# Order of the two kinds of score products, and of the gating layers, in an attention and routing pipeline

## The reference, cut to what matters

```python
x = x + tanh(g_xattn) * attention(layernorm(x), ctx, ctx)   # 32 query heads, 8 key/value heads, 16 wide
x = x + tanh(g_ffn)   * experts(layernorm(x))               # 8 experts, the best 2 of each token
# attention: softmax(q k^T / 4) v, softmax over the 128 context rows
# experts:   logits = tanh(x Wg1^T) Wg2^T; top 2, softmax of the two; silu(x Wup^T + bup) Wdown^T + bdown
```

## Time and profile before

| | |
|---|---|
| runs | 796.14, 796.16, 802.58 us; median 796.16 |
| profiled execution | 791.42 us, span 789.6 us |
| PE busy | 675.6 us, 86% of the span |
| DVE busy | 551.0 us, 70% |
| ACT busy | 380.1 us, 48% |
| POOL busy | 293.7 us, 37% |
| chain that ended last | PE 69%, DVE 14%, DMA 8%, POOL 3%, issue 3% |
| mean granted clock of PE | 0.946 of full speed |

### The profile page before, as it was taken

How to read it: one execution, slowest core, us unless ns; L and a number is a source line. 1 busy time by engine, 2 the same in 40 slices (tenths; PEclk the granted TensorE clock), 3 DMA queues, 4 the chain that set the end, 5 groups by cost and what they waited for, 6 DMA issues and landing times.

```text
span 789.6 us, 17887 instructions
## 1 busy us (share of the span) xinstructions
PE 675.6 (86%) x5232; PEld 463.6 (59%) x5232; DVE 551.0 (70%) x1541; ACT 380.1 (48%) x706; POOL 293.7 (37%) x406
## 2 busy tenths in 40 slices
PE   3789999999999999998889699999999998979600
PEld 2445545455455554554443488889998997768500
DVE  3567878778787787878873466777766766766635
ACT  2366766666676666766653133333333334433300
POOL 4123445454454545545432400000000026665564
PEclk9999999999999999999996689999999999898955
DMA  4622434344443443434221754444456468999898
GB/s 152 211 84 88 140 129 137 125 141 137 129 138 123 141 137 127 137 126 139 71 104 54 271 189 155 151 144 156 145 167 201 148 228 270 312 326 305 280 350 277
DMA packets 67847, 135.15 MB, mean 171 GB/s; under 512 B 8640, under 2 KB 12736, under 8 KB 67520
## 3 DMA queue, kind: packets, MB, share of 16 engines
q1 hardware_dynamic: 46432, 81.28, 30.8%
q0 software_dynamic: 10240, 33.56, 12.4%
q10 hardware_dynamic: 11104, 19.42, 8.0%
HBM read 76.04 MB, written 58.20 MB: 170 GB/s over the span
## 4 chain that ended last, share of the span: by engine, by line
PE 69%; DVE 14%; DMA 8%; POOL 3%; issue 3%; ACT 1%; DVEq 0%; SPq 0%; POOLq 0%
PE s_ps L987 12%; DVE nmax L770 10%; PE bank_a L966 8%; PE st_ps L1010 7%; DMA r_in<-x_scratch 5%; PE st_ps L1120 4%; PE st_ps L1121 4%; PE st_ps L1122 4%; PE bank_c L1027 4%; PE s_ps L1104 4%; DMA out<-r_in 3%; PE bank_b L975 3%; PE st_ps L1018 2%; POOL y_late L514 2%; PE bank_b L1133 2%
## 5 line engine op out<-in xcount | busy, mean ns | idle before, releaser
L770 DVE TENSOR_REDUCE nmax<-s_ps 128x8 f32<-128x1024 f32 x128 | 156.2, 1220 | 83.7 <-PE s_ps L987 83.3
L545 ACT ACTIVATE probs<-st_ps 128x1024 f32<-128x1024 f32 x128 | 131.2, 1025 | 109.7 <-PE st_ps L1018 106.1
L987 PE MATMUL s_ps<-k_t,q_t 32*128 32x256 f32 x1024 | 151.6, 414 | 35.4 <-DVE nmax L770 32.7
L1010 PE MATMUL st_ps<-q_t,k_t 32*128 32x512 f32 x512 | 147.9, 652 | 0.8 <-ACT probs L545 0.7
L987 PEld LDWEIGHTS s_ps<-k_t,q_t 32*128 32x128 f32 x1024 | 92.1, 191 | 86.0 <-DVE nmax L770 47.3
L493 POOL DMA_INDIRECT y<-expert_out,rows_all x42 | 41.3, 983 | 193.1 <-DMA expert_out<-y_sb 183.4
L1120 PE MATMUL st_ps<-w_hi,zh 128*128 x312 | 96.0, 308 | 0.6 <-DVE zl L891 0.6
L1121 PE MATMUL st_ps<-w_lo,zh 128*128 x312 | 88.9, 285 | 0.0
L1122 PE MATMUL st_ps<-w_hi,zl 128*128 x312 | 88.6, 284 | 0.0
L629 ACT ACTIVATE t_sb<-u_sb 128x256 f32<-128x256 f32 x78 | 32.6, 418 | 104.5 <-DVE u_sb L899 104.5
L470 POOL DMA_INDIRECT slots<-z,slot_i x64 | 64.2, 1004 | 16.4 <-issue 16.1
(11 more groups left out here) (149 smaller groups left out, 1420.3 us busy)
## 6 DMA issues: line engine op xcount, KB each, us to landing
expert_out<-y_sb SPq DMA_DIRECT2D x78, 256.0 KB, 2.8
z_s<-slots ACTq DMA_DIRECT2D x74, 256.0 KB, 2.7
x_in<-in_x SPq DMA_DIRECT2D x32, 256.0 KB, 2.7
wst<-in_w SPq DMA_DIRECT2D x32, 256.0 KB, 2.6
x_res<-in_x SPq DMA_DIRECT2D x32, 256.0 KB, 2.9
x_scratch<-x_res SPq DMA_DIRECT2D x32, 256.0 KB, 2.0
r_in<-x_scratch SPq DMA_DIRECT2D x21, 256.0 KB, 4.6
out<-r_in SPq DMA_DIRECT2D x21, 256.0 KB, 4.5
```

The costliest lines, as they stand in the source:

```text
L545: a.activation(out, st_ps[:, :].rearrange("t (k n) -> t k n", k=2), ACT.Exp, scale=HD ** -0.5).then_inc(exp_done[half], 1)
L770: v.tensor_reduce(out, s_ps[:, :].rearrange("s (r g c t) -> s r g c t", r=2, g=2, c=2), X_AXIS, ALU.max, negate=True).then_inc(max_done, 1)
L987: last = t_.matmul(s_ps[:, HALF * rr + 2 * P * gg:HALF * rr + 2 * P * (gg + 1)], q_t[r2][row:row + ROWS32, P * g_:P * (g_ + 1)], k_t[r2][r ...
L1010: t_.matmul(st_ps[:, HALF * rr:HALF * (rr + 1)], k_t[r][row:row + ROWS32, P * i:P * (i + 1)], q_t[r][row:row + ROWS32, :], start=True, sto ...
```

## The change

In `scores(j)` the two bf16 products of L1018 come first into `st_ps`, the fp32 products of L1010 follow and raise `st_done`, and `part(1)` is last. The first gating layer moves from between `scores(0)` and `scores(1)` to between `scores(1)` and `scores(2)`, behind the counting matmuls, and the second gating layer from there to behind `scores(2)`. ACT's tanh moves behind the exponential and the output copy that followed it. DVE's copy of the logits moves from ahead of `maxima(2)` to behind `z`, and the top 8 behind the reciprocals of the sums.

```diff
 # ACT
                     a.activation(nm_t[p3_][:, :], bank_q[:, :].bitcast(BF16)[:, 0:D], ACT.Copy).then_inc(nmt_copied, 1)
+                if valid(b4):
+                    exps(b4, 1, 1)
+                    o_out(b4, 0)
                 if valid(b6):
                     act.wait_ge(lg1_done, b6 + 1)
                     wait(act, lg2_done, b6)
                     a.activation(th_sb[:, :], bank_c[0:E, 0:S], ACT.Tanh).then_inc(th_done, 1)
-                if valid(b4):
-                    exps(b4, 1, 1)
-                    o_out(b4, 0)
 # DVE
                     v.bn_aggr(mv_o[:, :], st_o[:, :]).then_inc(o_mv, 1)
-                if valid(b6):
-                    dve.wait_ge(lg2_done, b6 + 1)
-                    v.tensor_copy(lg_sb[p6_][:, :], bank_c[:, 0:E]).then_inc(lg_copied, 1)
                 if valid(b2):
                     maxima(2)
...
-                if valid(b6):
-                    dve.wait_ge(lg_copied, b6 + 1)
                 if valid(b5):
                     dve.wait_ge(o_rs, b5 + 1)
                     v.tensor_scalar(z[q5][:, :], x_res[p5_][:, :], mv_o[:, 0:1], rs_o[:, :], ALU.subtract,
                                     ALU.mult).then_inc(z_done, 1)
                 if valid(b6):
-                    v.max(top8[:, :], lg_sb[p6_][:, :]).then_inc(top_done, 1)
+                    dve.wait_ge(lg2_done, b6 + 1)
+                    v.tensor_copy(lg_sb[p6_][:, :], bank_c[:, 0:E]).then_inc(lg_copied, 1)
+                if valid(b6):
+                    dve.wait_ge(lg_copied, b6 + 1)
                 if valid(b4):
                     weights_sum(b4, 0)
+                if valid(b6):
+                    v.max(top8[:, :], lg_sb[p6_][:, :]).then_inc(top_done, 1)
 # PE, scores(j)
                         for rr in range(2):
                             row = ROWS32 * (2 * over + rr)
-                            t_.matmul(st_ps[:, HALF * rr:HALF * (rr + 1)],
-                                      k_t[r][row:row + ROWS32, P * i:P * (i + 1)],
-                                      q_t[r][row:row + ROWS32, :], start=True, stop=False, tile_position=(row, 0))
+                            t_.matmul(st_ps[:, HALF * rr:HALF * (rr + 1)], pick[i][row:row + ROWS32, :],
+                                      nm_t[p][row:row + ROWS32, :], start=True, stop=False,
+                                      tile_position=(row, 0))
+                        for rr in range(2):
+                            row = ROWS32 * (2 * over + rr)
+                            last = t_.matmul(st_ps[:, HALF * rr:HALF * (rr + 1)],
+                                             k_t[r][row:row + ROWS32, P * i:P * (i + 1)],
+                                             q_t[r][row:row + ROWS32, :], start=False, stop=True,
+                                             tile_position=(row, 0))
+                        last.then_inc(st_done[over], 1)
                     if valid(b2):
                         part(1).then_inc(s_done, 1)
-                    if valid(b):
-                        for rr in range(2):
-                            row = ROWS32 * (2 * over + rr)
-                            last = t_.matmul(st_ps[:, HALF * rr:HALF * (rr + 1)], pick[i][row:row + ROWS32, :],
-                                             nm_t[p][row:row + ROWS32, :], start=False, stop=True,
-                                             tile_position=(row, 0))
-                        last.then_inc(st_done[over], 1)
 # PE, step
                 scores(0)
-                if valid(b6):
-                    pe.wait_ge(zt_copied, b6 + 1)
-                    for c in range(DC):
-                        last = t_.matmul(bank_c[0:E, 0:S], wg1[:, c * E:(c + 1) * E], z_t[:, P * c:P * c + P],
-                                         start=(c == 0), stop=(c == DC - 1))
-                    last.then_inc(lg1_done, 1)
...
                     t_.matmul(bank_b[:, E:2 * E], ones_b[:, :], m12[p7_][:, :], start=True,
                               stop=True).then_inc(rank_done, 1)
                 if valid(b6):
+                    pe.wait_ge(zt_copied, b6 + 1)
+                    for c in range(DC):
+                        last = t_.matmul(bank_c[0:E, 0:S], wg1[:, c * E:(c + 1) * E], z_t[:, P * c:P * c + P],
+                                         start=(c == 0), stop=(c == DC - 1))
+                    last.then_inc(lg1_done, 1)
+                scores(2)
+                if valid(b6):
                     pe.wait_ge(th_done, b6 + 1)
                     t_.matmul(bank_c[:, 0:E], th_sb[:, :], wg2[:, :], start=True, stop=True).then_inc(lg2_done, 1)
-                scores(2)
                 if valid(b4):
```

## The result

The changed kernel takes 817.18 us in the median against 796.15 us for the kernel before; the ratio of the times is 1.0162, with a 95% interval of 1.0082 to 1.0242. It is slower. The forecast was +0.6%. Two of the four runs of the changed kernel, 822.70 and 824.19 us, fell in a slower state, so the ratio compares the fast runs of both kernels; 1.0162 times 796.15 is 809.05 us. The profiled execution took 807.24 us (span 805.5) against 791.42 us (span 789.6), +15.8 us where the sum had said +4.8.

The account below looks back on a forecast made before the run. PE was taken as nearly the bound, with two intervals following the loop through DVE's maximum. +0.11 a step, +2.8 us over 25 steps, and the other steps gave +4.8; set against the timed median, 801 us, range 790 to 810.

Parts of the forecast that it names:

- rival A: In scores(j), the exposed bf16 load costs as much as the fp32 one: 808.6 us, 1.6% slower, chance 0.17.
- What releases the maximum: In scores(j), the semaphore on part(1) rises only once the fp32 products earlier in PE's list are through.
- interval 1 to 2: From scores(1) to scores(2): the loop through DVE's maximum grows, the first gating layer hides in a wait; 2.63 us, +0.13.
- rival B: DVE's maximum isn't held up by the earlier products, so the three +0.13 go: 790.1 us, 0.8% faster, chance 0.13.
- The exposed bf16 load: In scores(j), the weight load of the bf16 product now in front was taken to expose 0.02 us, against 0.11 for fp32.
- Interval 0 to 1: From scores(0) to scores(1): the first gating layer leaves and PE waits for the split of the maxima; -0.59 us.
- Rival C: The time freed between scores(0) and scores(1) is lost to another wait: 815.8 us if wholly lost, chance 0.07.
- Interval 2 to 3: From scores(2) to scores(3): the second gating layer enters and PE waits for DVE's later copy of the logits; +0.44 us.
- Interval 3 to 0: From scores(3) to the next scores(0): same loop through DVE's maximum, nothing moved; +0.13 us.
- Edit 1: The new order of products within scores(j): DVE's maximum starts 0.13 us later wherever it is waited for.
- The other steps: Outside the 25 full steps: +2.0 us in the last three steps with maxima, +0.5 in two early ones.
- rival D: PE idles more within a step, so the slow-clock part may move: 1 to 3 us either way, no case of its own.

Follow-up runs that it names:

- e9: The changed kernel once more, unedited, on the chip of a later batch: 821.30 us, ratio 1.0334 to the kernel before.
- e1: The kernel before with only the new order of the products in scores(j), gating layers not moved: 796.34 us, ratio 1.0027.
- e7: The changed kernel with GpSimd's second indirect transfer moved to the end of its step: 808.90 us, ratio 1.0161.
- e3: The changed kernel with one more tiny GpSimd operation ahead of the two indirect transfers: 803.28 us, ratio 1.0190.
- e6: The changed kernel with the copy of the logits directly behind the maximum of scores(2), new score order kept: 786.14 us, ratio 0.9900.
- e4: The changed kernel with the old order in scores(j) and the copy of the logits directly behind maxima(2): 781.86 us, ratio 0.9891.
- e8: The kernel before with a second tiny GpSimd operation ahead of the two indirect transfers: 790.52 us, ratio 0.9948.

## Why the prediction was too low

The change was forecast at 801 us, within 1% of no change; it is 1.6% slower, for which "slower by over 1%" had a chance of 0.28. The 809.05 us of the ratio lie just inside the range of 790 to 810, and that is luck: the range reached so high only to take in rival A (808.6), which is refuted below. The median of all four runs, 817, and the 821.30 of e9 lie outside. No rival is what happened.

**What releases the maximum: right.** e1 and the changed kernel have +0.15 in interval 1 to 2 in all 25 steps, against +0.13. Where nothing is late, the maximum of scores(3) starts 1.37 behind the first L987, and 1.36 was forecast, with 1.23 for rival B and 1.45 for rival A. This refutes B. The Trainium skill (TensorE: Matmul & The Clock Gate, Part 3) has matmuls in strict order at both ends. What agrees with that here is the semaphore, which rises only when the earlier-listed products are through. The ends of the records, which are modelled, don't keep the order: in scores(2) of the kernel before, L987 ends at 314.94, ahead of the earlier-listed L1010 at 315.04. So the prediction's "agrees on the end" holds for the semaphore alone.

**The exposed bf16 load: right.** From 322.08 to 322.31 are 0.23, that is 0.21 of columns and 0.02 of load. Rival A had 0.11 and is refuted. The group of these loads, for the earlier trace rows, has 90 ns each, half of the fp32 ones:

```profile
L1015 PEld LDWEIGHTS st_ps<-q_t,k_t 32*128 32x128 f32 x400 | 39.1, 188 | 0.0
...
L1010 PEld LDWEIGHTS st_ps<-nm_t,pick 32*128 32x128 bf16 x200 | 10.2, 90 | 0.0
```

The Trainium skill's bare rule (TensorE: Matmul & The Clock Gate, LDWEIGHTS), columns over 1.2 GHz (107 ns), doesn't fit either kind; its table on fast weight load, in the section on weight-path perf modes, points the right way.

**Interval 0 to 1: right** at 2.99 where nothing is late, with the wait of L1027 for L780 at 0.32 to 0.7. Rival C is refuted. In three steps the interval is 3.33 to 3.39, for DVE's split (L778) starts 0.24 to 0.29 later there, with nothing in the trace that it waits for. e7 has the same three, with its second transfer elsewhere, so this isn't the late semaphore.

**Interval 2 to 3: mis-sized.** Forecast +0.44, measured +0.65. The copy of the logits ended where I had it, behind L823. But L1062 starts 0.15 behind its end, not 0.06, and from L1062 to scores(3) it is 0.81, not 0.69. A wait that blocks doesn't explain it by itself, for L1027 and L987 block as well and start 0.06 behind DVE's end; why this list is slower is open. 0.2 in 25 steps is 5 us.

**Interval 3 to 0: the step that failed.** Forecast +0.13, measured +0.82 in 16 of 25 steps, 0.69 x 16 = 11 us more than forecast. The prediction said that SP's queue is touched only through a `slot_i` 0.4 later, "in a step in which POOL idles 6 us", and took that as free. POOL's time was free. The place was not. `slot_i` (L836) follows the wait for the logits and gives GpSimd's two transfers their start. Edit 1 makes the semaphore of scores(3) due later, and the intervals around `slot_i` shift too. The distance from the last L987's end to the second transfer goes from 0.41 to 0.20, that to DVE's start, if the semaphore is on time, from 0.09 to 0.24, and the two coincide. e3 (later start, all but four steps) and e7 (second transfer elsewhere, all steps) both bring the interval back to 2.65 with everything else in place, and e6 does so as a side effect. So for the 16 steps of the changed kernel, the place of the second transfer is shown as the cause. It isn't the whole of it: e1, e3, e4 and e6 keep three to five steps each in which DVE starts 0.34 to 0.88 behind the last L987, where on time is 0.24 (in e4, 0.09).

**Where it isn't settled.** What exactly is held, and by what. In the changed kernel the maximum isn't late in 3 of the 19 steps in which the transfer starts 0.11 to 0.20 behind the last L987, and in e9 not in 5 of 19. More than the critical semaphore is late: of the 64 recorded rises of the semaphores of L987, L1079 and L975 that were due near or in the second transfer (25 steps), 62 are late. 23 of them came 0.68 to 0.76 behind the transfer's start, the other 39 came 1.43 to 1.57 behind it, none between. In the kernel before, none of 67 rises of PE in the same place is late, though two of three kinds were due inside the transfer; with the transfers 0.36 later (e8) L975's are. Why is open.

A load beside the transfer isn't enough: the context load lands around the end of L987 in e7 too, where DVE is on time. It may be needed, though. In the last two steps with such a transfer (scores(3) at 403.44 and 419.25) no context load lands, the transfer starts 0.20 behind the last L987, and DVE is on time. Nor is it settled whether the recording takes part: in 7 of the 9 on-time steps the trace lacks the rise of the semaphore of L987, in the late ones it never does. Whether another GpSimd instruction would do the same wasn't tried.

**The other steps.** The last three with maxima and the early ones cost 6.9 us together where +2.5 was forecast, 4.7 of them behind the 25 steps and 2.1 ahead. Waits for L780 rose behind the 25 steps from 2.6 to 5.8 us; that it is because the tables delay a longer chain is argued, not shown. And the clock fell to its lower level three times ahead of the last scores(3), at 38.7, 393.7 and 410.8; in the kernel before it first fell at 414.6. At 393.7 PE had just waited 2.12 us for L780, at 38.7 it had waited 1.48 for the maximum. In e1 such a stretch cost 1.6 us each time. Every kernel with the gating layers moved has 0.85 to 0.96 behind its 25 steps, the kernel before, e1 and e8 have 1.00.

**The clock (rival D): size too small.** The rest of the program took between 373.9 and 391.3 us in two profiles of one kernel. I had allowed 1 to 3. Rival D looked for the cause in PE's idle time within a step. The early falls just named are in line with that. They don't account for the 17 us between two profiles of one kernel; the cause of those is open.

**Sum.** 2.8 forecast for the steps + 5 (2 to 3) + 11 (3 to 0) = 18.8, measured 18.9 (18.85). With 6.87 outside them: 25.7. The clock took back 9.8 in the profiled execution, and nothing of the kind is to be counted on in the median.

## What to carry to other kernels

When an instruction moves, ask not only whether its engine has time, but what it sets off and what else happens in that tenth of a microsecond: here an indirect GpSimd transfer and the one semaphore on the critical loop met, and cost 11 us. A tiny consumer that another engine waits for goes directly behind its producer's release; three lines made a loss (1.6%, and 3.3% in e9) a 1% gain (e6). Without the new order of the products (e4) the last scores(3) came 5.8 us earlier still, while the ratios, 0.9891 and 0.9900, don't tell the two apart. Compare such kernels up to a fixed instruction ahead of the stretch with a throttled clock, and read the clock of what lies ahead of it too; the total hid a 10 us difference in e1 and in e3, and of e1's, 3.2 us were the clock. A total that agrees with a sum proves little until its intervals do.

## What the hardware showed that I had not expected

- PE's semaphore can be held while PE runs on: in the changed kernel DVE saw it 0.93 behind the last L987 instead of 0.24, tied to the start of an indirect transfer of GpSimd (+0.76), in 16 of 25 steps. The late rises of PE's semaphores fall in two groups, 0.68 to 0.76 and 1.43 to 1.57 behind that start.
- A DVE operation of 8 columns with bf16 output took 1.57 us instead of 0.26, starting inside an indirect transfer and ending with the GpSimd operation behind it (e7).
- Behind its wait for the logits, PE starts 0.15 after the producer's end and needs 0.81 for a list that took 0.69 before; behind other waits that block (L1027, L987) it starts 0.06 after the producer's end.
- The clock fell to its lower level inside phase 1 for single short stretches, 1.6 us lost each time in e1, in kernels in which PE idles more.
- The granted clock of the last 380 us varied from 0.87 to 0.93 between profiles of one kernel, worth 17 us.
